# A four-stage transformer kernel: bias rows in four row groups, attention factors by row block, later waits in the delta stage

## The chip, the cores and the metric

The kernel runs on one NeuronCore of a Trainium2 chip. The core has five engines that run their own instruction streams and meet at semaphores: TensorE (PE; its weight loads are listed as PEld), VectorE (DVE), ScalarE (ACT), GpSimd (POOL) and SyncE (SP), which here only issues DMAs. The metric is the device time of one launch in microseconds (us), lower is better. Everything is fp32.

## The reference

The input is 2048 tokens of 512 numbers. Four residual layers follow each other, each on a layer-normalized input:

```python
x = x + attention_a(layernorm(x))   # channel attention: 512 x 512 scores
x = x + ffn(layernorm(x))           # six routed experts weighted by softmax of the top 6 of 8, plus a shared expert
x = x + attention_b(layernorm(x))   # gated delta rule with causal convolutions, 16 heads of 128
x = x + ffn(layernorm(x))           # the same weights again

# attention_a
attn_scores = einsum('bes,bfs->bef', qT, kT) / sqrt(16); softmax over f; @ vT; transpose; @ Wo
# ffn, last lines
eo = einsum('tnh,nhd->tnd', h, Wdown) + bdown
routed_out = einsum('tnd,tn->td', eo, w)
share = silu(xf @ Ws_up + bs_up) @ Ws_down + bs_down
```

## The kernel before

Each layer is a stage with its own semaphores; between stages all engines meet at a barrier. The order of the work on each engine is written out by hand in one block per engine, and each engine runs it strictly in that order.

**Attention factors** (`attention_stage`, from L215). Attention over channels needs no scores over tokens: the norm stage has accumulated the Gram matrix of the normalized input in PSUM banks 4 to 7, its upper triangle only. ScalarE copies the triangle out (L298), TensorE transposes the six missing 128 x 128 blocks (L270), ScalarE copies these (L301). Then come four products of 512 x 512 by 512 x 512, each as 4 x 4 matmuls of 128 x 512: `T1 = G Wk`, `S = Wq^T T1`, softmax over rows to `P`, `R1 = P^T Wo`, `M = Wv R1`. `product` (L260) has the output block `e` outside and the contraction block `k` inside, so one output bank after another is finished. ScalarE copies each finished bank to SBUF (L304, L311, L314); VectorE takes the row maxima of S (L321 to L323), ScalarE the exponentials (L307), VectorE scales by the reciprocal sums (L326, L328). Each product waits until all four blocks of its input are in SBUF (`pe.wait_ge(..., KC)`). Last, M is applied to the 16 token tiles (L291).

**Expert stages** (`ffn_stage`, L338, run twice). The 2048 tokens go through in FN = 4 blocks of 512. For each block there are 16 units: four chunks of the shared expert, then six experts of two chunks. `up(v)` (L428, L432) makes gate and up projections of unit v, ScalarE and VectorE form the hidden tile, `down(v - 1)` (L450) accumulates into PSUM banks 4 to 7, one bank for each 128 tokens. After the last unit of a block four more matmuls add the bias rows (L457): their contraction runs over 7 rows only, the six routed weights of a token and a row of ones, against `bdown` (six expert biases and the shared one). VectorE then adds the four banks to the residual (L552). TensorE's order at such a boundary is: shared up of the next block (its first unit), last down, four bias matmuls, shared up of the next unit, first down of the next block, which waits for the adds (`acc_read`). There are eight bias groups, three in the middle of each expert stage and one at each end.

**Delta stage** (`delta_stage`, L666). SyncE first issues the loads in this order: `xt` (first 512 tokens, transposed), `wab`, four projection weights `wqkv`, `wfb`, `par`, `dconst`, `onw`, then the second `xt`, `wgb`, `wo`, `xr`. GpSimd clears five buffers (L784 to L788) and signals `const_ready` after the last. TensorE waits for `const_ready` and `dconst` before its first matmul, which is `fa`, the low-rank decay projection (L1448, from `xt` and `wab`); ScalarE waits for `par` (L810) before it can copy `fa` out (L865); then TensorE makes the decay projection (L1442, from `wfb`) and the first q, k, v projections (L1367). The stage's loop runs over 16 units of 16 slots, with preparation two units ahead.

Of the kernel before, what the change touches and what calls it, by code (L numbers as in the profile page):

```python
# [8 lines left out]
ACT = mybir.ActivationFunctionType  # L9
# [224 lines left out]
def attention_stage(nc, x_sb, xnt, ps, cst, dram, ahead, meanvar):  # L234
# [3 lines left out]
    with ExitStack() as c2:  # L238
# [12 lines left out]
        with nc.Block() as block:  # L251
# [8 lines left out]
            def _(pe):  # L260
                def product(banks, lhs, rhs, signal):
                    for e in range(KC):
                        for k in range(KC):
                            last = pe.matmul(ps[:, banks + e, :], lhs[:, k, e * P:(e + 1) * P], rhs[:, k, :],
                                             start=(k == 0), stop=(k == KC - 1))
                        last.then_inc(signal, 1)
                for e in range(1, KC):
                    pe.wait_ge(g_upper, e)
                    for f in range(e):
                        last = pe.transpose(ps[:, e, f * P:(f + 1) * P], g[:, f, e * P:(e + 1) * P], cst[:, K_ID:K_ID + P])  # L270
                    last.then_inc(g_turned, 1)
                pe.wait_ge(w_in["wk"], 16)
                pe.wait_ge(g_upper, KC)
                pe.wait_ge(g_ready, KC - 1)
                product(0, g, w["wk"], t1_ps)
                pe.wait_ge(w_in["wq"], 16)
                pe.wait_ge(t1_ready, KC)
                product(4, w["wq"], t1, s_ps)
                pe.wait_ge(w_in["wo"], 16)
                pe.wait_ge(p_ready, KC)  # L280
                product(0, pr, w["wo"], r1_ps)
                pe.wait_ge(w_in["wvt"], 16)
                pe.wait_ge(r1_ready, KC)
                product(4, w["wvt"], r1, m_ps)
# [11 lines left out]
            def _(act):  # L296
                for e in range(KC):
                    act.activation(g[:, e, e * P:D], ps[:, 4 + e, e * P:D], ACT.Copy).then_inc(g_upper, 1)  # L298
                for e in range(1, KC):
                    act.wait_ge(g_turned, e)  # L300
                    act.activation(g[:, e, 0:e * P], ps[:, e, 0:e * P], ACT.Copy).then_inc(g_ready, 1)  # L301
# [37 lines left out]
def ffn_stage(nc, tag, x_sb, xnt, ps, cst, dram, store_to, wg, wu, wgu_in, meanvar=None):  # L339

    with ExitStack() as c2:
# [10 lines left out]
        bd = sb("bdown", [NR + 1, D])  # L352
        wt = sb("weights_t", [NE, T])
# [12 lines left out]
        names = ("w_in", "wr_in", "wd_in", "wsu_in", "wsd_in", "wt_out", "order", "logits_ps", "logits_out", "logits_turned", "logits_max",  # L366
                 "exp_ready", "probs_ready", "wt_ps", "wt_ready", "acc_ps", "acc_read", "stored", "gated")
        (w_in, wr_in, wd_in, wsu_in, wsd_in, wt_out, order, logits_ps, logits_out, logits_turned, logits_max, exp_ready, probs_ready, wt_ps,
# [11 lines left out]
        with nc.Block() as block:  # L380

            @block.sync
            def _(sp):
# [3 lines left out]
                for dst, name in ((bg, "bgate"), (bu, "bup"), (bs, "bsup"), (bd, "bdown")):  # L387
                    sp.dma_start(dst[:], dram[name]).then_inc(w_in, 16)
                sp.dma_start(wsd[:], dram["wsdown"]).then_inc(wsd_in, 16)
# [1209 lines left out]
```

## Time and profile before

| | |
|---|---|
| median of three runs | 3613.39 us (3612.41 to 3616.37) |
| the profiled execution | 3611.68 us, span 3609.6 us |
| granted TensorE clock, mean | 0.972 of full speed |
| TensorE busy | 3428.2 us, 95% of the span |
| VectorE, ScalarE busy | 1886.7 us (52%), 1434.1 us (40%) |
| matmuls of the bias rows, L457 | 64 records, 30.5 us busy |
| attention stage | from 57.6 to 186 us |
| expert stages | from 202.5 to 840 us and from 2971.8 us to the end |
| delta stage | from 861.2 to 2940.9 us |

"Busy" is the time in which at least one instruction of the engine ran. Each fp32 matmul stands in the trace as two records (4 bias matmuls are "x8"). "Granted clock" is the share of full TensorE speed; 1.00 is 2.4 GHz and 0.50 is 1.2 GHz. A name behind "<-" in brackets says what ended an idle time.

### The profile page before, as it was taken

The page shows a single profiled execution, that of the slowest core. Times are in us where ns is not written, and L with a number is a line of the kernel's source. Part 1 is how long each engine was busy: PE and PEld are TensorE (multiplying, and loading weights), DVE is VectorE, ACT ScalarE, POOL GpSimd, SP SyncE. Part 2 cuts the span into 40 slices and gives each one's busy share as a digit, 9 for nine tenths or more (in the row PEclk, how much of TensorE's full clock was granted, in tenths as well). Part 3 has the DMA queues.
Part 4 walks back from the last instruction along what each step waited for, and adds up shares of the span by engine and source line. Part 5 has one row for each costly group of instructions (what it writes and reads, how often), then busy time and mean ns, then how long its engine had stood idle before and what let it go on. Part 6 is the DMA issues. An engine that isn't in the chain of part 4 may idle for free. (4 is left out here: it accounts for less than half of the span.)

```text
span 3609.6 us, 85178 instructions
## 1 busy us (share of the span) xinstructions
PE 3428.2 (95%) x37232; PEld 1644.9 (46%) x37232; DVE 1886.7 (52%) x3186; ACT 1434.1 (40%) x3321; POOL 125.2 (3%) x457
## 2 busy tenths in 40 slices
PE   7989999996789999999999999999999869999999
PEld 4444444443344444454545454444445434444444
DVE  2221111113787888788877878887888431111111
ACT  2020000003357656766675676567666521000000
POOL 0000000000000000000000000000000000000000
PEclk9999999998889999999999999999999969999999
DMA  4030100004101111121111211111211032100000
GB/s 166 0 96 0 29 29 0 12 0 151 34 26 37 46 55 37 41 65 41 31 65 38 63 34 49 40 39 39 67 40 35 17 144 80 29 0 29 0 12 12
DMA packets 83725, 156.21 MB, mean 43 GB/s; under 512 B 8782, under 2 KB 33998, under 8 KB 79516
## 3 DMA queue, kind: packets, MB, share of 16 engines
q1 hardware_dynamic: 83356, 150.77, 12.9%
q8 instruction: 295, 4.83, 0.5%
q14 instruction: 74, 0.61, 0.1%
HBM read 133.71 MB, written 17.04 MB: 42 GB/s over the span
## 5 line engine op out<-in xcount | busy, mean ns | idle before, releaser
L1367 PE MATMUL psum<-dl_xt,dl_wqkv 128*128 128x512 f32 x1536 | 779.0, 625 | 9.6 <-DVE dl_qkv L1010 9.6
L541 DVE SCALAR_TENSOR_TENSOR f_act_g<-psum,f_bup,f_act_g 128x512 f32<-128x512 f32 x96 | 72.1, 751 | 929.8 <-ACT f_act_g L495 929.8
L1010 DVE SCALAR_TENSOR_TENSOR dl_qkv<-psum,dl_par,dl_qkv 128x511 f32<-128x511 f32 (+2 forms) x576 | 428.6, 744 | 39.0 <-ACT dl_tails L857 32.0
L495 ACT ACTIVATE f_act_g<-psum,f_bgate 128x512 f32<-128x512 f32 x96 | 66.0, 687 | 923.1 <-PE psum L432 923.1
L1367 PEld LDWEIGHTS psum<-dl_xt,dl_wqkv 128*128 128x128 f32 x1536 | 258.6, 190 | 249.7 <-issue 213.8
L432 PE MATMUL psum<-xnt_sb,wup 128*128 128x512 f32 x768 | 345.3, 593 | 0.0
L428 PE MATMUL psum<-xnt_sb,wgate 128*128 128x512 f32 x768 | 345.3, 593 | 0.0
L450 PE MATMUL psum<-f_wdown,f_hidden 128*128 128x512 f32 x768 | 345.0, 593 | 0.0
L1374 PE MATMUL psum<-dl_wo,dl_sg 128*128 128x512 f32 x512 | 261.0, 624 | 0.4 <-DVE dl_sg L1214 0.4
L853 ACT ACTIVATE dl_qkv<-psum,dl_par 128x512 f32<-128x512 f32 x192 | 148.8, 775 | 218.6 <-PE psum L1367 218.2
L428 PEld LDWEIGHTS psum<-xnt_sb,wgate 128*128 128x128 f32 x768 | 146.2, 190 | 183.4 <-issue 183.4
L450 PEld LDWEIGHTS psum<-f_wdown,f_hidden 128*128 128x128 f32 x768 | 146.2, 190 | 183.4 <-issue 183.4
L432 PEld LDWEIGHTS psum<-xnt_sb,wup 128*128 128x128 f32 x768 | 146.1, 190 | 183.4 <-issue 183.4
L1099 DVE TENSOR_TENSOR dl_kq<-dl_kq,dl_dec 128x512 f32<-128x512 f32 x320 | 206.9, 688 | 3.9 <-PE psum L1417 3.9
L823 ACT ACTIVATE dl_sdec<-dl_alt,dl_tot 128x128 f32<-128x128 f32 x512 | 162.5, 392 | 60.3 <-DVE dl_alt L1004 60.3
L838 ACT ACTIVATE dl_ubuf<-psum 128x128 f32<-128x128 f32 x256 | 70.4, 275 | 273.3 <-PE psum L1336 273.3
L823 ACT ACTIVATE dl_sdec<-dl_state,dl_tot 128x128 f32<-128x128 f32 x512 | 162.8, 395 | 21.8 <-DVE dl_state L1004 21.8
L1004 DVE TENSOR_TENSOR dl_alt<-dl_sdec,psum 128x512 f32<-128x512 f32 x128 | 87.5, 684 | 151.2 <-PE psum L1347 151.0
L1347 PE MATMUL psum<-dl_ubuf,dl_kkt 32*128 32x128 f32 x2048 | 132.3, 328 | 17.4 <-ACT dl_ubuf L838 17.4
L1417 PEld LDWEIGHTS psum<-dl_kq,dl_qkv 128*32 128x32 f32 x10240 | 106.9, 112 | 88.2 <-issue 82.3
L1004 DVE TENSOR_TENSOR dl_state<-dl_sdec,psum 128x512 f32<-128x512 f32 x128 | 87.5, 683 | 107.3 <-PE psum L1347 106.3
L997 DVE SCALAR_TENSOR_TENSOR dl_rbuf<-psum,dl_nkap,dl_val 128x128 f32<-128x128 f32 x256 | 87.9, 343 | 101.7 <-PE psum L1309 101.7
(200 smaller groups left out, 4494.0 us busy)
## 6 DMA issues: line engine op xcount, KB each, us to landing
dl_wqkv<-in_dw_qkv SPq DMA_DIRECT2D x192, 256.0 KB, 2.6
dl_wo<-in_dwo SPq DMA_DIRECT2D x16, 1024.0 KB, 6.2
f_weights_b<-f_weights_by_expert SPq DMA_DIRECT2D x48, 256.0 KB, 6.3
wgate<-in_wgate SPq DMA_DIRECT2D x2, 3072.0 KB, 19.3
wup<-in_wup SPq DMA_DIRECT2D x2, 3072.0 KB, 24.4
f_wdown<-in_wdown SPq DMA_DIRECT2D x2, 3072.0 KB, 13.0
x_sb<-in_x SPq DMA_DIRECT2D x4, 1024.0 KB, 9.2
x_after_experts<-x_sb SPq DMA_DIRECT2D x16, 256.0 KB, 2.0
```

Of the source, the lines that this page charges most:

```text
L428: last = pe.matmul(ps[:, 2 * b, :], lhs, xnt[:, k, s * FT:(s + 1) * FT], start=(k == 0), stop=(k == KC - 1))
L432: last = pe.matmul(ps[:, 2 * b + 1, :], wu[:, n, k, c * P:(c + 1) * P], xnt[:, k, s * FT:(s + 1) * FT], start=(k == 0), stop=(k == KC - 1))
L450: last = pe.matmul(ps[:, 4 + i, :], hid[:, b, i * P:(i + 1) * P], rhs, start=(u == 0), stop=False)
L823: last = act.activation(sdec[:, j, :], heads_state(k, sl)[:, j, :], ACT.Copy, scale=tot(k)[:, j, sl:sl + 1])
L853: act.activation(qkv[:, a, j, :], ps[:, bank, :], ACT.Identity, bias=par[:, h, 12 + a:13 + a], scale=par[:, h, 4 * a + 3:4 * a + 4])
L1004: dve.tensor_tensor(heads_state(k, sl + 1), sdec[:, :, :], ps[:, 0:HJ, 0:P], ALU.add).then_inc(s["s_read"], 1)
L1010: tap_ = lambda dl: dve.scalar_tensor_tensor(y_[:, dl:TT], ps[:, bank, 0:TT - dl], par[:, h, 4 * a + 3 - dl:4 * a + 4 - dl], y_[:, dl:TT], ...
L1099: o.done(dve.tensor_tensor(late, late, dv[:, :, :, 0, 0:1].broadcast_to([P, HJ, nb, m]), ALU.mult))
L1347: last = pe.matmul(ps[:, j, 0:P], kkt(k)[part(j), sl, :], ubuf[part(j), sl % 2, :], start=True, stop=True)
L1367: last = pe.matmul(ps[:, bank, :], wq[:, n % RING, m, :], xt[:, u // HG % 2, m, :], start=(m == 0), stop=(m == KC - 1))
L1374: last = pe.matmul(ps[:, bank, :], sg[:, m, P * i:P * i + P], wo[:, m, :], start=(m == 0), stop=(m == HJ - 1))
L1417: last = pe.matmul(ps[part(j), bank, C * g:C * g + C], chunk(qkv[:, KK], g)[:, j, :], rhs, start=True, stop=True)
```

## The change

Three edits, each in a stage of its own.

1. Expert stages: `bdown` and the transposed routing weights are loaded four times, to partitions 0, 32, 64 and 96, and bias matmul i takes its 7 rows from group i. ScalarE waits for three small loads instead of four; TensorE waits for the eight loads (`bd_in`) before the first bias group. SyncE issues three more `bdown` and three more `weights_t` DMAs per stage.
2. Attention: `product` does one contraction block k for all four banks at a time, and each k waits only for its own block of the input. The transposes of G move behind the wait for `wk`, between the blocks of the first product, and use bank 4.
3. Delta stage: SyncE waits for `xt` and `wab` to land before it issues the other loads; `const_ready` and `dconst` are waited for where they are used (TensorE from iteration k = -1 on); a new `tails_ready` covers the first cleared buffer alone.

```diff
@@ attention_stage, tensor engine
-                def product(banks, lhs, rhs, signal):
+                def product(banks, lhs, rhs, k, signal):
                     for e in range(KC):
-                        for k in range(KC):
-                            last = pe.matmul(ps[:, banks + e, :], lhs[:, k, e * P:(e + 1) * P], rhs[:, k, :],
-                                             start=(k == 0), stop=(k == KC - 1))
-                        last.then_inc(signal, 1)
-                for e in range(1, KC):
+                        last = pe.matmul(ps[:, banks + e, :], lhs[:, k, e * P:(e + 1) * P], rhs[:, k, :],
+                                         start=(k == 0), stop=(k == KC - 1))
+                        if k == KC - 1:
+                            last.then_inc(signal, 1)
+
+                def turn(e):
                     pe.wait_ge(g_upper, e)
                     for f in range(e):
-                        last = pe.transpose(ps[:, e, f * P:(f + 1) * P], g[:, f, e * P:(e + 1) * P], cst[:, K_ID:K_ID + P])
+                        last = pe.transpose(ps[:, 4, P * f:P * f + P], g[:, f, e * P:(e + 1) * P], cst[:, K_ID:K_ID + P])
                     last.then_inc(g_turned, 1)
                 pe.wait_ge(w_in["wk"], 16)
-                pe.wait_ge(g_upper, KC)
-                pe.wait_ge(g_ready, KC - 1)
-                product(0, g, w["wk"], t1_ps)
+                for k in range(KC):
+                    pe.wait_ge(g_upper, k + 1)
+                    if k > 0:
+                        pe.wait_ge(g_ready, k)
+                    if k + 1 < KC:
+                        turn(k + 1)
+                    product(0, g, w["wk"], k, t1_ps)
                 pe.wait_ge(w_in["wq"], 16)
-                pe.wait_ge(t1_ready, KC)
-                product(4, w["wq"], t1, s_ps)
+                for k in range(KC):
+                    pe.wait_ge(t1_ready, k + 1)
+                    product(4, w["wq"], t1, k, s_ps)
...
@@ ffn_stage
-        bd = sb("bdown", [NR + 1, D])
-        wt = sb("weights_t", [NE, T])
+        bd = sb("bdown", [P, D])
+        wt = sb("weights_t", [P, T])
...
+                for i in range(4):
+                    sp.dma_start(bd[32 * i:32 * i + NR + 1, :], dram["bdown"]).then_inc(bd_in, 16)
...
+                for i in range(4):
+                    sp.dma_start(wt[32 * i:32 * i + NE, :].rearrange("e (i t) -> e i t", t=P),
+                                 wt_dram.rearrange("i e t -> e i t")).then_inc(bd_in, 16)
...
                         if s == 0:
-                            pe.wait_ge(w_in, 16 * 5)
+                            pe.wait_ge(bd_in, 16 * 8)
                         for i in range(4):
-                            pe.matmul(ps[:, 4 + i, :], wt[0:NR + 1, s * FT + i * P:s * FT + (i + 1) * P], bd[:, :],
+                            rows = slice(32 * i, 32 * i + NR + 1)
+                            pe.matmul(ps[:, 4 + i, :], wt[rows, s * FT + i * P:s * FT + (i + 1) * P], bd[rows, :],
                                       start=False, stop=True).then_inc(acc_ps, 1)
@@ delta_stage, sync engine
                 sp.dma_start(xt[:, 0], xnt_dram[0]).then_inc(s["xt_in"], 16)
                 sp.dma_start(wab[:], d["dwa"]).then_inc(s["wab_in"], 16)
+                sp.wait_ge(s["xt_in"], 16)
+                sp.wait_ge(s["wab_in"], 16)
                 for n in range(RING):
                     load_proj(n)
@@ delta_stage, GpSimd; ScalarE and VectorE wait for tails_ready in place of const_ready at their start
-                pool.memset(tails[:], 0.0)
+                pool.memset(tails[:], 0.0).then_inc(s["tails_ready"], 1)
@@ delta_stage, tensor engine
-                pe.wait_ge(s["const_ready"], 1)
-                pe.wait_ge(s["dc_in"], 16)
                 for k in range(-2, UNITS + 1):
                     run = 0 <= k < UNITS
+                    if k == -1:
+                        pe.wait_ge(s["const_ready"], 1)
+                        pe.wait_ge(s["dc_in"], 16)
```

TensorE's stream in the attention stage, one piece of the difference (`at_t` is T1, `at_g` is G, `at_pr` is P, `at_r` is R1; 128x128 is a transpose):

```order
-L270 MATMUL psum<-constants_sb,at_g 128x128 x6
-L264 MATMUL psum<-at_wk,at_g 128x512 x16
-L264 MATMUL psum<-at_t,at_wq 128x512 x16
-L264 MATMUL psum<-at_wo,at_pr 128x512 x16
-L264 MATMUL psum<-at_r,at_wvt 128x512 x16
-L291 MATMUL psum<-at_m,xnt_sb 128x512 x64
+L271 MATMUL psum<-constants_sb,at_g 128x128
+L263 MATMUL psum<-at_wk,at_g 128x512 x4
+L271 MATMUL psum<-constants_sb,at_g 128x128 x2
+L263 MATMUL psum<-at_wk,at_g 128x512 x4
+L271 MATMUL psum<-constants_sb,at_g 128x128 x3
+L263 MATMUL psum<-at_wk,at_g 128x512 x8
```

The six transposes now stand between the row blocks of the first product; the counts of matmuls are the same.

SyncE's stream at the start of the delta stage, with waits, before. A semaphore of this stage is printed under the name that its number bore in an earlier stage, where there was one.

```order
L728 DMA dl_xt<-xn_transposed 128x2048
L729 DMA dl_wab<-in_dwa 128x1088
L726 DMA dl_wqkv<-in_dw_qkv 128x512 x4
L732 DMA dl_wfb<-in_dwfb 128x512
L733 DMA dl_par<-in_dheads 128x272
```

And now (`n1_std_ready` is here the semaphore of `wab`):

```order
L741 DMA dl_xt<-xn_transposed 128x2048
L742 DMA dl_wab<-in_dwa 128x1088
L739 DMA dl_wqkv<-in_dw_qkv 128x512 [waits n1_std_ready,dl_xt_in]
L739 DMA dl_wqkv<-in_dw_qkv 128x512 x3
L747 DMA dl_wfb<-in_dwfb 128x512
L748 DMA dl_par<-in_dheads 128x272
```

Twelve loads that were queued at once (four `wqkv`, then eight others) stand behind a wait now, `wfb` and `par` among them.

TensorE's stream at the same place, with waits, before (`n1_var_ready` stands for `wab`, `n1_xn_ready1` for `dconst`, `n1_dve_order` for `const_ready`):

```order
L1448 MATMUL psum<-dl_xt,dl_wab 128x512 [waits n1_var_ready,dl_xt_in,n1_xn_ready1,n1_dve_order]
L1448 MATMUL psum<-dl_xt,dl_wab 128x512 x3
L1442 MATMUL psum<-dl_fa,dl_wfb 128x512 [waits dl_read6,dl_wfb_in]
L1442 MATMUL psum<-dl_fa,dl_wfb 128x512 [waits dl_read6]
L1367 MATMUL psum<-dl_xt,dl_wqkv 128x512 [waits dl_w_in0,dl_xt_in]
```

And now:

```order
L1465 MATMUL psum<-dl_xt,dl_wab 128x512 [waits dl_xt_in,n1_std_ready]
L1465 MATMUL psum<-dl_xt,dl_wab 128x512 x3
L1459 MATMUL psum<-dl_fa,dl_wfb 128x512 [waits dl_read6,dl_wfb_in]
L1459 MATMUL psum<-dl_fa,dl_wfb 128x512 [waits dl_read6]
L1384 MATMUL psum<-dl_xt,dl_wqkv 128x512 [waits dl_w_in0,dl_xt_in]
```

The first matmul waits for its two operands alone; `dconst` and the cleared buffers are waited for later.

## Rows read from the trace of the kernel before

**Rows 1.** windows: stretch, length, busy us (instructions) by engine, granted clock, DMA share, GB/s
```profile
202.50:840.00 637.50, 630.32 (x1477) 276.15 (x1477) 101.10 (x159) 48.73 (x69) 0.00 (x0) 0.99 0.08 25
```

**Rows 2.** timeline (start us, us, engine, operation, tiles), TensorE, a boundary between token blocks
```profile
3135.78 3.70 PE L457 MATMUL psum<-f_bdown,f_weights_t 7*128 7x512 f32 x8
3139.41 5.40 PE L428 MATMUL psum<-xnt_sb,f_wsup 128*128 128x512 f32 x8
3144.64 3.60 PE L450 MATMUL psum<-f_wsdown,f_hidden 128*128 128x512 f32 x8
```

**Rows 3.** timeline, TensorE, another boundary, first expert stage
```profile
683.69 3.70 PE L428 MATMUL psum<-xnt_sb,f_wsup 128*128 128x512 f32 x8
687.23 3.60 PE L450 MATMUL psum<-f_wsdown,f_hidden 128*128 128x512 f32 x8
```

**Rows 4.** windows, columns as in rows 1, behind three bias groups of the first expert stage
```profile
367.90:374.70 6.80, 6.80 (x9) 2.52 (x8) 4.49 (x11) 0.00 (x0) 0.00 (x0) 0.50 0.62 172
528.30:531.70 3.40, 3.40 (x5) 1.35 (x4) 2.66 (x8) 0.00 (x0) 0.00 (x0) 0.50 0.50 152
683.70:690.00 6.30, 6.30 (x16) 2.95 (x16) 3.75 (x9) 0.69 (x1) 0.00 (x0) 1.00 0.33 122
```

**Rows 5.** timeline, TensorE, one state step of the delta stage and its successor
```profile
1770.24 0.50 PE L1347 MATMUL psum<-dl_ubuf,dl_kkt 32*128 32x128 f32 x8
1770.68 1.12 PE L1374 MATMUL psum<-dl_wo,dl_sg 128*128 128x512 f32 x2
```

**Rows 6.** timeline, VectorE: a PSUM add and successor; first output add behind rows 2
```profile
132.17 0.69 DVE L332 TENSOR_TENSOR x_sb<-psum,x_sb 128x512 f32<-128x512 f32 x1 [34.99 <-PE psum L291]
132.89 0.69 DVE L334 BATCH_NORM_STATS2 at_stats<-x_sb 128x6 f32<-128x512 f32 x1
...
3136.94 0.69 DVE L552 TENSOR_TENSOR x_sb<-psum,x_sb 128x512 f32<-128x512 f32 x1 [9.08 <-PE psum L457]
```

**Rows 7.** timeline, TensorE: first down projection of the first expert stage
```profile
217.33 3.24 PE L450 MATMUL psum<-f_wsdown,f_hidden 128*128 128x512 f32 x7 [0.16 <-DVE f_logits L519]
```

**Rows 8.** timeline, TensorE, the factors of the attention stage
```profile
58.31 1.20 PE L270 MATMUL psum<-constants_sb,at_g 128*128 128x128 f32 x6 [2.38 <-ACT at_g L298]
62.86 16.28 PE L264 MATMUL psum<-at_wk,at_g 128*128 128x512 f32 x32 [3.35 <-DMA at_wk<-in_wk]
79.92 13.97 PE L264 MATMUL psum<-at_t,at_wq 128*128 128x512 f32 x32 [0.78 <-ACT at_t L304]
97.32 15.67 PE L264 MATMUL psum<-at_wo,at_pr 128*128 128x512 f32 x32 [3.44 <-DVE at_pr L328]
113.77 13.97 PE L264 MATMUL psum<-at_r,at_wvt 128*128 128x512 f32 x32 [0.78 <-ACT at_r L311]
```

**Rows 9.** timeline, VectorE, softmax: last maximum, first and last scaling
```profile
93.92 0.69 DVE L321 TENSOR_REDUCE at_mx<-psum 128x1 f32<-128x512 f32 x1 [2.55 <-PE psum L264]
...
94.91 0.49 DVE L328 TENSOR_SCALAR at_pr<-at_pr,at_rc 128x512 f32<-128x512 f32 x1
...
96.69 0.49 DVE L328 TENSOR_SCALAR at_pr<-at_pr,at_rc 128x512 f32<-128x512 f32 x1
```

**Rows 10.** delta stage start: timelines of four engines, transfer window, landing of dl_xt
```profile
871.55 0.23 ACT L810 ACTIVATE dl_nega<-dl_par 128x16 f32<-128x16 f32 x1 [8.96 <-DMA dl_par<-in_dheads]
...
872.26 5.75 PE L1448 MATMUL psum<-dl_xt,dl_wab 128*128 128x512 f32 x8 [17.54 <-DMA dl_dconst<-in_dconst]
878.87 1.96 PE L1442 MATMUL psum<-dl_fa,dl_wfb 128*128 128x512 f32 x4 [0.86 <-ACT dl_fa L865]
...
861.31 0.33 SPq L728 DMA_DIRECT2D dl_xt<-xn_transposed  x1
...
863.00:865.00 2.00, 0.00 (x0) 0.00 (x0) 0.00 (x0) 0.00 (x0) 2.00 (x3) 0.50 0.93 385
...
DMA to landing us min/median/max: 4.9/7.1/9.3
...
865.10 0.53 POOL L788 MEMSET dl_xcr<- 128x512 f32 x1
```

More of the change, by code:

```diff
@@ L279, in _ @@
                 pe.wait_ge(w_in["wo"], 16)
-                pe.wait_ge(p_ready, KC)
-                product(0, pr, w["wo"], r1_ps)
+                for k in range(KC):
+                    pe.wait_ge(p_ready, k + 1)
+                    product(0, pr, w["wo"], k, r1_ps)
                 pe.wait_ge(w_in["wvt"], 16)
-                pe.wait_ge(r1_ready, KC)
-                product(4, w["wvt"], r1, m_ps)
+                for k in range(KC):
+                    pe.wait_ge(r1_ready, k + 1)
+                    product(4, w["wvt"], r1, k, m_ps)
@@ L300, in _ @@
                     act.wait_ge(g_turned, e)
[L301 removed]
+                    act.activation(g[:, e, 0:e * P], ps[:, 4, 0:e * P], ACT.Copy).then_inc(g_ready, 1)
                 for e in range(KC):
@@ L365, in ffn_stage @@
         cmp_a, cmp_b = (wb[:, 0, 2 * n:2 * n + 2, :].rearrange("p a (b c d) -> p (a b) c d", c=NE, d=NE) for n in range(2))
-        names = ("w_in", "wr_in", "wd_in", "wsu_in", "wsd_in", "wt_out", "order", "logits_ps", "logits_out", "logits_turned", "logits_max",
+        names = ("w_in", "bd_in", "wr_in", "wd_in", "wsu_in", "wsd_in", "wt_out", "order", "logits_ps", "logits_out", "logits_turned", "logits_max",
                  "exp_ready", "probs_ready", "wt_ps", "wt_ready", "acc_ps", "acc_read", "stored", "gated")
-        (w_in, wr_in, wd_in, wsu_in, wsd_in, wt_out, order, logits_ps, logits_out, logits_turned, logits_max, exp_ready, probs_ready, wt_ps,
+        (w_in, bd_in, wr_in, wd_in, wsu_in, wsd_in, wt_out, order, logits_ps, logits_out, logits_turned, logits_max, exp_ready, probs_ready, wt_ps,
          wt_ready, acc_ps, acc_read, stored, gated) = (sem(tag + n) for n in names)
@@ L386, in _ @@
                 sp.dma_start(wsu[:], dram["wsup"]).then_inc(wsu_in, 16)
-                for dst, name in ((bg, "bgate"), (bu, "bup"), (bs, "bsup"), (bd, "bdown")):
+                for dst, name in ((bg, "bgate"), (bu, "bup"), (bs, "bsup")):
                     sp.dma_start(dst[:], dram[name]).then_inc(w_in, 16)
+                for i in range(4):
+                    sp.dma_start(bd[32 * i:32 * i + NR + 1, :], dram["bdown"]).then_inc(bd_in, 16)
                 sp.dma_start(wsd[:], dram["wsdown"]).then_inc(wsd_in, 16)
@@ L483, in _ @@
                 act.activation(act_g[:, 0, :], ps[:, 4, :], ACT.Copy).then_inc(logits_out, 1)
-                act.wait_ge(w_in, 16 * 4)
+                act.wait_ge(w_in, 16 * 3)
                 for v in range(ALL):
@@ L699, in delta_stage @@
         b_dram = nc.dram_tensor("betas", [H, TT], F32).ap()
-        names = """const_ready wab_in par_in onw_in dc_in kps r_ready u_ps u_ready s_ps s_read sd_ready o_ps o_read o_squared tapped
+        names = """tails_ready const_ready wab_in par_in onw_in dc_in kps r_ready u_ps u_ready s_ps s_read sd_ready o_ps o_read o_squared tapped
             bnd_ready edged q_silu k_silu v_silu k_square q_square softplus_abs softplus_exp softplus_ln series_done softplus_sum decay_ready
@@ L813, in _ @@
                 act.wait_ge(s["nega_ready"], 1)
-                act.wait_ge(s["const_ready"], 1)
+                act.wait_ge(s["tails_ready"], 1)
                 def decay_state(k, sl):
@@ L818, in decay_state @@
                     if sl == 0:
+                        act.wait_ge(s["const_ready"], 1)
                         act.wait_ge(s["tot_ready"], k + 1)
@@ L986, in _ @@
                 step = lambda ins: (o.done(ins), o.wait())
-                dve.wait_ge(s["const_ready"], 1)
+                dve.wait_ge(s["tails_ready"], 1)
                 dve.wait_ge(s["dc_in"], 16)
@@ L1109, in level_take @@
                         wait_full(dve, "level", u, 0)
+                        dve.wait_ge(s["const_ready"], 1)
                         dve.tensor_copy(waited[:, 1:2], cst[:, K_ONE:K_ONE + 1])
```

1 line of the change is left out of this document (removed).

## The prediction

> **What bounds the kernel now.** I read the windows by stage first: in the first expert stage TensorE is busy 630 of 637.5 us at a granted clock of 0.99 [rows 1], and the second stands the same, so there every matmul that takes less time shortens the run one for one, and so does a stretch at half clock. Then the timeline at the edges, where work of TensorE is thin or absent: the boundary between two blocks of tokens [rows 2 to 4], the attention factors [rows 8, 9] and the start of the delta stage [rows 10]. The reader is to see three things. At a boundary the four bias matmuls (8 records) take as long as four full ones, though only 7 of the 128 rows work, and in five of six boundaries the following shared up projection takes longer than 3.5 us, 5.2 in the rows shown. In the attention stage TensorE stands still before each product, longest, 3.44 us, for the softmax. In the delta stage it starts only when `dconst` has landed, a table it doesn't use there.
>
> **Bias groups.** From the first bias record to the next projection a group takes 3139.41 - 3135.78 = 3.63 us [rows 2]. Records of a full matmul follow each other in 3.43 / 8 = 0.43 us (8 records from 683.69 to 687.23 are 3.54, with 0.11 of start). If four row groups run side by side, two record times stay and six go: 3.63 - 6 x 0.43 = 1.05 us. Do they? The trace has the case with 128 columns in place of 512: a state step sends four matmuls with 32 rows each to four banks, 8 records, and the next operation starts 0.44 us after the first of them [rows 5]. A record of 128 columns takes a quarter of 0.43, 0.107 us; one after the other the 8 would need 0.86. So they overlap fully, with about 0.2 us for the start and end. I take 1.07 us, a gain of 2.56 a group. The other bound is that accumulating groups go one by one: gain 0.
>
> In the middle of a stage (6 groups) the whole gain counts if the adds keep up. The first add starts 1.16 us after the first bias record in the old order (3136.94 behind 3135.78) [rows 2, 6]; the four banks are now complete at that same moment, and PSUM adds follow each other in 0.72 us (132.17 to 132.89) [rows 6], so they are done by 1.16 + 3 x 0.72 + 0.69 = 4.0 us. The next down projection, which overwrites the banks one each 0.86 us, comes one shared up (3.43) behind the group, at 4.5 us. It doesn't wait. 6 x 2.56 = 15.4 us.
>
> At the end of a stage (2 groups) the adds are the chain: the last began 3 x 0.86 us behind the first, paced by the matmuls, and begins 3 x 0.72 behind it now, 0.4 us sooner, 0.8 in both. Bias groups: 16.2 us.
>
> The Trainium skill speaks against counting the full factor (TensorEngine Tiling, PSUM Bottleneck: behind a fourfold speedup of TensorE, the copies out of PSUM may become the bound). By it the six inner groups would gain little; the row pitch of 0.72 us agrees at the two ends only.
>
> The added loads hide: the three more `bdown` issues come before `wsdown`, at some 0.45 us each, but the first down projection that needs it is released by VectorE's logits [rows 7]; without that cover they would cost 1.4 us per stage. The `weights_t` copies are wanted 100 us later. Nothing is taken for them.
>
> **The clock behind the bias groups.** Behind the first group of the first expert stage the granted clock is 0.50 for 6.8 us, behind the second for 3.4 us, behind the third it stays at 1.00 [rows 4]. Half clock for x us costs x / 2: 5.1 us together. In the second expert stage all three fall, as the one shown: 3144.64 - 3139.41 = 5.23 us against 3.54 without a fall [rows 2, 3], 1.7 each, 5.1. Since 3.6 us of seven-row matmuls is sometimes not enough for a fall, I expect none behind 1.07 us. Gain 10.2 us; bounds 0 and 10.2.
>
> The Trainium skill (TensorE: Matmul & The Clock Gate, What's actually happening) has the gate follow how busy TensorE has been. Read literally, the bias groups are busy all the time and the fall isn't theirs. The rows speak against this: each fall stands right behind seven-row matmuls. Were the page's reading right, the 10.2 us would stay lost.
>
> **Attention.** G's blocks are ready long before `wk` lands (the transposes end at 59.5, the product starts at 62.86, released by the load) [rows 8], so starting the first product on a part of G gains nothing, and the six transposes, which were hidden, now stand behind the load. They took 1.20 us with their waits; I take 0.8 for them back to back, partly at half clock (bounds 0.6 and 1.2): a loss.
>
> The second and fourth product each waited 0.78 us (plus a start of about 0.15) for the last copy [rows 8]. With k outside, the four banks finish 0.86 us apart in the last block, each copy is shorter than that, and the next product needs only the first. Gain 2 x 0.93 = 1.9.
>
> The softmax: the last bank is finished at 93.9 as before, but the other three only 2.6, 1.7 and 0.9 us earlier, so VectorE has a queue: four rounds of maximum and negation of 0.92 us each (0.69 + 0.15 and two starts), beginning at 91.35, end at 95.0. Then the first reciprocal and scaling, ready 0.6 us on, at 95.6, and the product may start on block 0 at 95.7; before, it needed the last scaling, which began at 96.69, and started at 97.32 [rows 8, 9]. Gain 1.6; the other scalings come 0.6 us apart, beneath blocks of 3.4 us. The old pause of 3.44 us was followed by a fall of the clock: the third product took 15.67 us, the second 13.97. A pause of 1.8 us should be survived more often than not; I take the 1.7 (bounds 0 and 1.7). Sum for the stage: 0.8 lost, 1.9 + 1.6 + 1.7 won: 4.4 us.
>
> **Delta stage.** `xt` lands 4.9 us after its issue at 861.3, at 866.2. `wab`, 0.56 MB behind it in the queue at 385 GB/s [rows 10], lands at 867.7. TensorE then starts `fa` at 867.8 and not at 872.26. Cold as before, it takes 5.75 us or up to one more: ready by 873.6 to 874.8.
>
> What is queued behind SyncE's new wait: twelve loads, and ScalarE waits for `par` before it can copy `fa` out. Before, `par` landed at 871.5, 10.2 us behind the first issue at 861.3, with 3.06 MB up to its end, 7.9 us at 385 GB/s; 2.3 us are latency. Now four `wqkv`, `wfb` and `par`, 1.45 MB, take 3.8 us behind 867.8, and with the latency `par` lands at 873.9. `nega` takes 0.5 us, so `fa` can be copied from 874.4, and with its own end in the middle of its range I take 874.6; the decay projection starts at 875.3, not at 878.87 [rows 10]. Gain 3.6 us, bounds 2.5 and 4.5. `par` is what is late next: without SyncE's wait the gain would be 0.5 more. Everything behind comes from that chain (the first convolution stood at 885 and needs `onw`, now at about 875.5) and moves with it. The last initial load lands 2 us later than before, some 8 us ahead of the first reuse of the `wqkv` ring. The last clearing ends at 865.6 [rows 10], so moving `const_ready` is worth nothing; the repeated waits are passed at once.
>
> **Sum.** 16.2 + 10.2 + 4.4 + 3.6 = 34.4 us. The profiled execution took 3611.7 us, so 3577.3; the median of the runs shown is 1.7 above it, so I predict 3579 us.
>
> **Rivals.**
> - *The clock still falls* (the bias groups or the softmax pause are not what drops it, or even the short ones are enough). For it: the pauses move but don't vanish. Against it: the third group of 3.6 us without a fall. 34.4 - 10.2 - 1.7 = 22.5 us: 3591.
> - *The row groups go one after another*, since they add to what stands in the banks, which the state step doesn't. Then groups cost 3.6 us and the clock falls: 34.4 - 26.4 = 8.0: 3605. Against it: four different banks, as in rows 5.
> - *The adds become the bound* inside the stages, by the page cited. The six inner groups would bring 0.4 us each like the ends, 13.0 less: 3592. Against it: adds need to begin 2.6 us later than in the sum before bank after bank is missed.
> - *Slower*: each change of row group empties the array and exposes the next weight load. A change of tiling costs about 0.1 us on each side; with weight load and fill it would be 0.6 us at all 8 records, 5.0 + 0.6 = 5.6 us a group in place of 3.6: 16 lost and not 16.2 won, and the longer thin stretch would keep the clock at half twice as long everywhere (another 6 to 10 lost, and the 10.2 not won). With the 8.0 of the rest: some 15 us slower, 3628. It decides from 4.6 us a group.
>
> **Chances and range.** Forecast 0.71, clock 0.13, adds 0.03, one by one 0.07, slower 0.03, others 0.03. The clock's falls in the delta stage depend on where pauses come to lie, and each is worth 1.7 us, so the forecast alone spans 3573 to 3586; with the clock rival the range is 3572 to 3593. What differs by under 0.2% (7.2 us) can't be told from no change. Faster: the first three and most of the fourth, 0.93; same 0.04; slower 0.03.
>
> **What would show it.** Bias groups: 8 records within 1.3 us, and the next shared up within 3.6 us of its start at all six boundaries. Attention: no idle before the second and fourth product, 1.8 us before the third. Delta stage: first matmul 4.4 us earlier against SyncE's first load, second projection 3.6. I am wrong if a bias group takes over 2 us, if the clock falls behind it, or if the delta stage does not shorten by 2.5 to 4.5 us from its first load to its end.

## The result and the profile after

The changed kernel takes 3578.04 us (median of 4 runs, 3575.09 to 3582.45) against 3612.9 us before, measured beside it (4 runs, 3610.29 to 3616.37): a ratio of 0.9903, 95% interval 0.989 to 0.9917. Measured once more it was 3579.93 us against 3613.2 us, ratio 0.9908 (0.9895 to 0.9922). The forecast was 3579 us. In the profiled executions the span goes from 3609.6 to 3580.5 us.

The timeline of TensorE in the changed kernel, at the first boundary between two blocks of tokens in the first expert stage and at the one that answers to [rows 2] (columns as there):

```profile
360.80 1.14 PE L470 MATMUL psum<-f_bdown,f_weights_t 7*128 7x512 f32 x8
361.87 3.70 PE L440 MATMUL psum<-xnt_sb,f_wsup 128*128 128x512 f32 x8
365.41 3.60 PE L462 MATMUL psum<-f_wsdown,f_hidden 128*128 128x512 f32 x8
...
3119.41 1.14 PE L470 MATMUL psum<-f_bdown,f_weights_t 7*128 7x512 f32 x8
3120.48 3.70 PE L440 MATMUL psum<-xnt_sb,f_wsup 128*128 128x512 f32 x8
```

A bias group now takes 1.07 us to the next projection, where [rows 2] has 3.63, and that projection takes 3.54 us (361.87 to 365.41) at the first place, where [rows 2] has 5.23. Windows behind three boundaries of the first expert stage, which answer to [rows 4]:

```profile
361.00:374.00 13.00, 13.00 (x37) 5.54 (x34) 5.54 (x12) 1.37 (x2) 0.00 (x0) 1.00 0.66 198
513.00:525.00 12.00, 12.00 (x34) 5.17 (x34) 5.55 (x12) 0.88 (x2) 0.00 (x0) 1.00 0.75 192
666.00:679.00 13.00, 13.00 (x37) 5.62 (x30) 5.54 (x12) 1.38 (x2) 0.00 (x0) 1.00 0.22 81
```

The granted clock is 1.00 in all of them. It fell at five of six boundaries before, at none now.

The gain in an expert stage can be read without the noise of the whole time. From the start of the first bias group of a stage to the start of its fourth it is 466.28 and 466.33 us before (365.24 to 831.52, 3135.78 to 3602.11) and 453.57 us in both stages now (360.80 to 814.37, 3119.41 to 3572.98): 12.7 and 12.8 us. Both stages of e1 and of e9 to e12, further executions with the same bias groups, take 453.57 us too.

VectorE's adds behind the last bias group, of before (first fence) and after:

```profile
3603.27 0.69 DVE L552 TENSOR_TENSOR x_sb<-psum,x_sb 128x512 f32<-128x512 f32 x1 [5.65 <-PE psum L457]
...
3605.84 0.69 DVE L552 TENSOR_TENSOR x_sb<-psum,x_sb 128x512 f32<-128x512 f32 x1 [0.17 <-PE psum L457]
```

```profile
3574.14 2.48 DVE L565 TENSOR_TENSOR x_sb<-psum,x_sb 128x512 f32<-128x512 f32 x4 [5.65 <-PE psum L470]
```

Before, the adds were paced by the matmuls, one each 0.86 us, and took 3605.84 + 0.69 - 3603.27 = 3.26 us; now four stand back to back in 2.48 us, a pitch of (2.48 - 0.69) / 3 = 0.60 us.

The attention factors on TensorE, which answer to [rows 8], and the two rows of VectorE that answer to [rows 9]:

```profile
63.44 0.47 PE L271 MATMUL psum<-constants_sb,at_g 128*128 128x128 f32 x1 [7.22 <-DMA at_wk<-in_wk]
63.71 5.77 PE L263 MATMUL psum<-at_wk,at_g 128*128 128x512 f32 x8
...
73.30 7.03 PE L263 MATMUL psum<-at_wk,at_g 128*128 128x512 f32 x16
80.17 13.90 PE L263 MATMUL psum<-at_t,at_wq 128*128 128x512 f32 x32
95.72 13.97 PE L263 MATMUL psum<-at_wo,at_pr 128*128 128x512 f32 x32 [1.66 <-DVE at_pr L336]
109.53 13.90 PE L263 MATMUL psum<-at_r,at_wvt 128*128 128x512 f32 x32
124.11 6.28 PE L299 MATMUL psum<-at_m,xnt_sb 128*128 128x512 f32 x14 [0.69 <-ACT at_m L322]
```

```profile
95.09 0.49 DVE L336 TENSOR_SCALAR at_pr<-at_pr,at_rc 128x512 f32<-128x512 f32 x1
...
96.87 0.49 DVE L336 TENSOR_SCALAR at_pr<-at_pr,at_rc 128x512 f32<-128x512 f32 x1
```

No row of the second or fourth product has idle time; the third starts 0.63 us behind the start of the first scaling and 1.15 us ahead of the last one. Its pause is 1.66 us and not 3.44, and it takes 13.97 us and not 15.67, so the clock didn't fall.

The start of the delta stage, which answers to [rows 10]: timelines of TensorE, ScalarE and SyncE, then windows of the transfers.

```profile
849.82 5.33 PE L1465 MATMUL psum<-dl_xt,dl_wab 128*128 128x512 f32 x8 [12.67 <-DMA dl_wab<-in_dwa]
858.65 2.45 PE L1459 MATMUL psum<-dl_fa,dl_wfb 128*128 128x512 f32 x4 [3.49 <-ACT dl_fa L881]
```

```profile
857.40 0.23 ACT L825 ACTIVATE dl_nega<-dl_par 128x16 f32<-128x16 f32 x1 [12.96 <-DMA dl_par<-in_dheads]
857.66 0.22 ACT L827 ACTIVATE dl_nega<-dl_nega 128x16 f32<-128x16 f32 x1
857.91 0.60 ACT L881 ACTIVATE dl_fa<-psum 128x512 f32<-128x512 f32 x1
```

```profile
843.15 0.33 SPq L741 DMA_DIRECT2D dl_xt<-xn_transposed  x1
843.53 0.43 SPq L742 DMA_DIRECT2D dl_wab<-in_dwa  x1
849.85 1.76 SPq L739 DMA_DIRECT2D dl_wqkv<-in_dw_qkv  x4
851.65 0.43 SPq L747 DMA_DIRECT2D dl_wfb<-in_dwfb  x1
852.12 0.43 SPq L748 DMA_DIRECT2D dl_par<-in_dheads  x1
```

```profile
851.00:853.00 2.00, 2.00 (x4) 0.85 (x3) 0.00 (x0) 0.00 (x0) 0.00 (x0) 0.50 1.03 289
853.00:855.00 2.00, 2.00 (x5) 0.57 (x3) 0.00 (x0) 0.00 (x0) 0.00 (x0) 0.96 0.77 236
855.00:857.00 2.00, 0.16 (x1) 0.00 (x0) 0.00 (x0) 0.00 (x0) 0.00 (x0) 1.00 0.90 305
```

TensorE starts early, as meant: 6.67 us behind SyncE's first load and not 10.95. But SyncE then stands until 849.85, ScalarE's first use of `par`, which comes right behind its landing, is only 14.25 us behind the first load (10.24 before), ScalarE has waited 12.96 us for it, and TensorE 3.49 us for ScalarE. The decay projection comes 15.50 us behind the first load, 17.56 before; the first convolution on VectorE, which is the end of this chain, at 23.50 and 23.86.

Where the time went, by windows of the whole run, cut at SyncE's first load of the delta stage and its last store, of before and after:

```profile
0.00:861.30 861.30, 811.78 (x2059) 372.77 (x2059) 170.47 (x315) 95.58 (x154) 0.20 (x4) 0.98 0.12 41
861.30:2935.40 2074.10, 1971.39 (x33632) 985.03 (x33632) 1607.27 (x2688) 1277.87 (x3077) 125.01 (x453) 0.97 0.14 45
2935.40:3609.60 674.20, 645.07 (x1541) 287.06 (x1541) 109.00 (x183) 60.65 (x90) 0.00 (x0) 0.97 0.12 41
```

```profile
0.00:843.10 843.10, 794.62 (x2059) 365.93 (x2059) 169.47 (x315) 96.11 (x154) 0.20 (x4) 0.98 0.13 42
843.10:2917.50 2074.40, 1972.73 (x33632) 985.78 (x33632) 1607.85 (x2688) 1278.68 (x3077) 124.99 (x453) 0.97 0.14 45
2917.50:3580.50 663.00, 630.68 (x1541) 281.24 (x1541) 107.96 (x183) 60.77 (x90) 0.00 (x0) 0.97 0.13 42
```

18.2 us were won ahead of the delta stage (attention, three bias groups inside the expert stage and one at its end), 11.2 behind it, and in the delta stage nothing: 2074.1 and 2074.4 us.

### The profile page after: what moved, and what is told of

The parts are those of the page before. It is cut to its first block and busy times, and to the rows that moved or that the text cites. A ratio compares the mean times of both kernels' runs of the same rounds, so it can differ in the third digit from the quotient of the medians.

```text
span 3580.5 us, 85211 instructions
## 1 busy us (share of the span) xinstructions
PE 3398.0 (95%) x37232; PEld 1633.0 (46%) x37232; DVE 1885.3 (53%) x3186; ACT 1435.6 (40%) x3321; POOL 125.2 (3%) x457
```

## The experiments

Theory: the bias groups (by their own time and by the clock) and the attention edit bring the time, as the forecast has it; the delta edit brings its 3.6 us, or its wait takes them back. The rivals of the forecast are tested with it. The kernel before was run beside each group of runs: 3612.51 us (27 runs) beside e1 to e4, 3612.31 (21 runs) beside e5 to e8, 3613.2 (9 runs) beside e9 to e12. Ratios are to these.

**The three parts alone.** e1 is the kernel before with the bias edit of the diff (L397, L413 and L469), e2 with the attention edit, e3 with the delta edit.

> The kernel before with the bias edit alone (four row groups). Theory: the row groups run side by side (8 records within 1.14 us, a group of 1.07 us in place of 3.63) and the clock no longer falls behind a group: 16.2 + 10.2 = 26.4 us less, 3586 to 3588. Rival 1, the clock gain comes from somewhere else than the bias groups: 16 us less, and the shared up projection behind a group takes 5.2 us at most boundaries. Rival 2, part of the gain is eaten by the added loads: under 24 us.

> The kernel before with the attention edit alone. Theory: 4.4 us less with the clock kept behind the softmax pause, 2.7 if it falls. The trace has no idle before the second and fourth product and 1.7 to 1.9 us before the third. Rival, the six transposes now behind the load of wk cost more than the overlap of the copies brings: 2 us less or nothing.

> The kernel before with the delta edit alone. The theory of the prediction: 3.6 us less. Rival, from the trace of the changed kernel: SyncE's wait holds par back, fa stands finished 3.5 us before ScalarE may copy it out, TensorE's clock falls in that pause, and the first convolution comes only 0.4 us earlier: 0 to 0.5 us less, and the delta stage as long as before (2074 us from its first load to its last store).

Measured: e1 3586.42 us (5 runs, ratio 0.9930, 0.9916 to 0.9944); e2 3608.37 (11 runs, 0.9992, 0.9983 to 1.0001); e3 3610.75 (11 runs, 0.9998, 0.9989 to 1.0006). The bias edit carries 26.1 us; from the first to the fourth bias group of a stage e1 takes 453.57 us in both stages, the same as the changed kernel. The attention edit's interval reaches from 6.1 us won to nothing, so the whole time doesn't show it. The traces do: the first bias group of the first expert stage, which has only the norm and the attention stage and the same expert work ahead of it, starts between 365.2 and 366.5 us in the seven profiled executions without the attention edit (before, e1, e3 to e6, e8) and between 360.4 and 362.4 in the four with it (e2, after, e9, e11): means 366.1 and 361.1, 5.0 us. The delta edit can't be told from none by the whole time, nor from the 3.6 us of the forecast: its interval reaches 4.0 us won. The product of the three ratios is 0.9920, 4 to 6 us short of the whole; the intervals are just wide enough for that.

**e4: the delta edit without SyncE's waits.** It keeps the rest of the delta edit.

```diff
-                sp.wait_ge(s["xt_in"], 16)
-                sp.wait_ge(s["wab_in"], 16)
                 for n in range(RING):
                     load_proj(n)
```

> The delta edit without SyncE's two waits (TensorE's wait for dconst and the cleared buffers still moved). If SyncE's wait is what took the gain: par lands 10.2 us behind the first load as in the kernel before, fa (ready 12.5 us behind it) is copied at once, the decay projection starts 4.1 us earlier than before, and the run is 3.5 to 4.5 us shorter. Rival, the start of the stage is not on the path at all, later work absorbs it: as e3, no gain.

Measured 3609.74 us (11 runs, 0.9992, 0.9983 to 1.0001): 2.8 us less than before, under the 3.5 to 4.5 expected and not shown by the time alone. TensorE's timeline in e3, then in e4 (SyncE's first load at 863.21 and 861.09):

```profile
869.87 5.95 PE L1452 MATMUL psum<-dl_xt,dl_wab 128*128 128x512 f32 x8 [13.83 <-DMA dl_wab<-in_dwa]
877.95 3.60 PE L1446 MATMUL psum<-dl_fa,dl_wfb 128*128 128x512 f32 x4 [2.13 <-ACT dl_fa L868]
```

```profile
867.74 5.64 PE L1450 MATMUL psum<-dl_xt,dl_wab 128*128 128x512 f32 x8 [13.39 <-DMA dl_wab<-in_dwa]
874.24 1.95 PE L1444 MATMUL psum<-dl_fa,dl_wfb 128*128 128x512 f32 x4 [0.87 <-ACT dl_fa L866]
```

Both start `fa` some 6.65 us behind the first load: the early start doesn't come from SyncE's wait. With the wait the second projection is 14.74 us behind the load and takes 3.60 us at half clock; without it 13.15 and 1.95. The first convolution on VectorE follows at 22.68 and 19.45 (23.86 in the kernel before).

**e5: the bias matmuls with all 128 rows.** One row group, `bd` and `wt` cleared to zero by GpSimd and filled in their first rows, so that the same four matmuls run over 128 rows one after the other. It tells whether thin work lets the clock fall, or the boundary itself.

```diff
-        bd = sb("bdown", [NR + 1, D])
-        wt = sb("weights_t", [NE, T])
+        bd = sb("bdown", [P, D])
+        wt = sb("weights_t", [P, T])
...
-                            pe.matmul(ps[:, 4 + i, :], wt[0:NR + 1, s * FT + i * P:s * FT + (i + 1) * P], bd[:, :],
+                            pe.matmul(ps[:, 4 + i, :], wt[:, s * FT + i * P:s * FT + (i + 1) * P], bd[:, :],
```

> The kernel before, but the bias matmuls contract over all 128 rows: bdown and weights_t are cleared to zero first and only 7 rows carry numbers; still one matmul after another. If seven-row work is what lets the clock fall: a group takes 3.43 us, no fall behind the six inner groups, the shared up projection behind it takes 3.43 us, and the run is 10.2 us plus 6 to 8 times 0.2 us shorter, 3600 to 3602. Rival, the fall comes from VectorE's adds, the DMAs or the boundary as such: falls stay at most of the boundaries and the run is 1 to 2 us shorter, 3611.

Measured 3600.38 us (4 runs, 0.9965, 0.9952 to 0.9979). TensorE's timeline at its first boundary:

```profile
366.48 3.60 PE L464 MATMUL psum<-f_bdown,f_weights_t 128*128 128x512 f32 x8
369.91 3.60 PE L435 MATMUL psum<-xnt_sb,f_wsup 128*128 128x512 f32 x8
```

The group is as long as a full projection, and the projection behind it is at full clock. No clock falls at any of the six boundaries of this kernel. The median is 11.9 us lower, with an interval from 7.6 to 17.3. The traces are sharper: from the first bias group to the fourth e5 takes 460.07 us in both stages, 6.2 and 6.3 less than before, 12.5 in all. Of these 10.2 are the clock (the stretches of [rows 4] and their like); the rest is 0.4 us for each boundary, since a group takes 3.43 us and not 3.63, and the projections on both sides of it 3.43 and not 3.53.

Over all profiled executions: the clock fell at 29 of the 36 inner boundaries of the six kernels with seven rows in one group (before, e2, e3, e4, e7, e8), and at none of the 48 of the eight kernels with four or two row groups or with 128 rows.

**e6: two row groups.** e1 with the banks on two row groups in turn.

```diff
-                            rows = slice(32 * i, 32 * i + NR + 1)
+                            rows = slice(32 * (i % 2), 32 * (i % 2) + NR + 1)
```

> The bias edit with two row groups in place of four (matmul i takes group i % 2). If the time goes by record times side by side: 8 records in four of them, a group of 3.63 - 4 x 0.43 = 1.9 us, 1.7 won at six places, some 0.6 at the two ends, and the clock kept: 3613 - 10.3 - 0.6 - 10.2 = 3591. Rival, the second matmul of a group waits for its own row group and blocks those behind it, so nothing overlaps beyond the first pair: 2.6 to 3 us a group, 3600. If the clock falls behind some of the groups of 1.9 us, 1.7 more for each.

Measured 3588.91 us (4 runs, 0.9937, 0.9922 to 0.9953). TensorE's timeline at the first boundary of e6:

```profile
366.37 1.99 PE L462 MATMUL psum<-f_bdown,f_weights_t 7*128 7x512 f32 x8
368.29 3.70 PE L432 MATMUL psum<-xnt_sb,f_wsup 128*128 128x512 f32 x8
```

One group costs 3.63 us (before), two 1.92, four 1.07, and neither of the last two is followed by a fall. The gain goes by row groups side by side, as the sum took it, and the median is 2 us under the 3591 expected, within its interval.

**e7: attention edit, transposes first.** e2 with the six transposes ahead of the wait for `wk`, each row of blocks in a bank of its own, and the product started on the whole of G.

```diff
+                for e in range(1, KC):
+                    pe.wait_ge(g_upper, e)
+                    for f in range(e):
+                        last = pe.transpose(ps[:, e, f * P:(f + 1) * P], g[:, f, e * P:(e + 1) * P], cst[:, K_ID:K_ID + P])
+                    last.then_inc(g_turned, 1)
                 pe.wait_ge(w_in["wk"], 16)
```

> The attention edit with the six transposes ahead of the wait for wk, as in the kernel before, and the contraction outside. Theory: the transposes are hidden again; from the first product to the application of M 59.8 us (65.6 before, 60.7 in the changed kernel with 0.3 more ahead of it), the run 0.8 us shorter than with the attention edit alone, 3607.5. Rival, the copies of G are late without the blocks between: as the attention edit alone.

Measured 3607.47 us (11 runs, 0.9987, 0.9978 to 0.9996), as expected; here the interval excludes no change. What the order of the transposes adds is another matter. `wk` lands at another time in each execution, so it has to be read from that landing. From there to the application of M, which took 65.6 us before, the versions with transposes behind the load take 61.1 us (e2), 60.7 (the changed kernel), 60.6 (e9) and 60.8 (e11), those with transposes first 59.7 (e7), 60.4 (e10) and 60.0 (e12): some 0.8 us less, which is the term of 0.8 in the forecast.

**e8: delta edit, parameters first.** e3 without SyncE's waits and with `par` and `wfb` right behind `wab`.

```diff
-                sp.wait_ge(s["xt_in"], 16)
-                sp.wait_ge(s["wab_in"], 16)
+                sp.dma_start(par[:], d["dheads"]).then_inc(s["par_in"], 16)
+                sp.dma_start(wfb[:], d["dwfb"][0]).then_inc(s["wfb_in"], 16)
                 for n in range(RING):
                     load_proj(n)
-                sp.dma_start(wfb[:], d["dwfb"][0]).then_inc(s["wfb_in"], 16)
-                sp.dma_start(par[:], d["dheads"]).then_inc(s["par_in"], 16)
```

> The delta edit without SyncE's waits and with par and wfb issued right behind wab. Par lands some 8 us behind the first load, fa is ready later than that, so its landing no longer matters and this is like the variant without waits: decay projection 13 us behind the first load, the run 3 us shorter than before, 3609 to 3610. Rival, the first projection weights come too late now: the first convolution comes over 20 us behind the first load, 3611.

Measured 3610.77 us (11 runs, 0.9994, 0.9985 to 1.0003). `par` is there 6.66 us behind the first load, yet the first convolution comes at 19.55 and not sooner than in e4 (19.45): once `par` lands by 10.4 us (e4), the end of `fa` is what is late, not `par`. Moving the small loads ahead brought nothing beyond taking the wait out.

**The changed kernel and two variants of it.** e9 is the changed kernel itself, e10 has the edit of e7 on top, e11 that of e8, e12 both.

> The changed kernel once more, unaltered, as the yardstick for the three versions timed beside it. Both theories: 3576 to 3580 us (3578.0 before). The product of the ratios of its three parts timed alone (0.9930, 0.9992, 0.9998) is 0.9920, or 3583 to 3584; if it lands there instead, the first timing was a lucky one; if it stays at 3578, the parts help each other by some 5 us or the bias part alone was timed high.

> The changed kernel with the transposes of its first attention product issued ahead of the wait for the weight wk, into banks of their own, and the four mirror copies with them. Theory that savings ahead of the first normalised tile carry to the end: the fourth product ends 2.0 to 2.5 us sooner than in the changed kernel, and the time is 1 to 2.5 us under the yardstick. Rival, that a later drop of the clock or a load takes it back: no difference (within 1 us).

> The changed kernel without SyncE's two waits ahead of the projection weights, and with the per-head parameters and the decay weights issued right behind the first loads. Theory that the start of the delta stage is a chain that its end follows: parameters 6.7 us behind the first load instead of 14.3, first convolution at 19.5 instead of 23.5, and 2 to 4 us off the time. Rival, that the stage is paced further on (by the state steps and by the clock): the first convolution as early, but under 1.5 us off the time. The same edit on the kernel before gave 1.5 us, so 1 to 2 us is taken.

> Both edits of the two runs beside it together: early transposes and the order of the delta loads without SyncE's waits. Theory that they add: 2 to 4.5 us under the yardstick, 3574 to 3576 us. Rival, that the phase of the clock decides at this size: the best of the four by less than 1 us, or not the best.

Measured: e9 3579.93 us (4 runs, 3577.28 to 3581.89), e10 3578.95 (5 runs, 3576.98 to 3582.24), e11 3575.29 (4 runs, 3574.94 to 3580.64), e12 3576.92 (4 runs, 3574.51 to 3578.64); ratios 0.9908, 0.9908, 0.9899 and 0.9900, each some 0.0014 either way. e10 missed: the fourth product starts 0.2 us sooner than in e9 and not 2 (the expectation had read an early landing of `wk` into the gain). e11 came out 4.6 us under e9 where 1 to 2 were expected. e11 and e12 have the lowest medians, but their intervals overlap with e9's, so by time alone neither is shown to beat the changed kernel, and the two edits don't visibly add. The start of e11 on TensorE and ScalarE:

```profile
855.89 1.95 PE L1457 MATMUL psum<-dl_fa,dl_wfb 128*128 128x512 f32 x4 [0.87 <-ACT dl_fa L879]
```

```profile
850.14 0.23 ACT L823 ACTIVATE dl_nega<-dl_par 128x16 f32<-128x16 f32 x1 [5.78 <-DMA dl_par<-in_dheads]
...
855.14 0.60 ACT L879 ACTIVATE dl_fa<-psum 128x512 f32<-128x512 f32 x1 [4.53 <-PE psum L1463]
```

ScalarE now waits for TensorE, not for the load, and the pause of TensorE is 0.87 us. What tells the versions apart better than the whole time is the length of the delta stage, from SyncE's first load to its last store, one execution each:

| start of the delta stage | executions | length, us |
|---|---|---|
| as before | before, e1, e2, e5, e6, e7 | 2074.0, 2073.3, 2077.3, 2078.0, 2072.7, 2073.0 |
| as changed, SyncE waits | after, e3, e9, e10 | 2074.4, 2074.1, 2075.9, 2070.4 |
| SyncE doesn't wait | e4, e8, e11, e12 | 2069.7, 2070.8, 2068.8, 2071.9 |

The same start varies by 5 us. The clock is one reason: one minus the granted clock, summed over windows of 2.5 us of the stage, is 49.7 us in e6, the shortest of the six with the start as before, and 60.6 in e5, the longest. The four stages without SyncE's wait are all shorter than these six (means 2070.3 and 2074.7, 4.4 us), and the clock accounts for little of it (the sums have means of 52.9 and 54.2). Those of the changed start, with a mean of 2073.7, are not all shorter.

## Why the prediction came out right, and where it didn't

**Bias groups: right inside the stages, not at the ends.** 1.07 us a group, as taken, so 6 x 2.56 = 15.4 us. With the clock the sum had 12.8 us for each stage; 12.7 and 12.8 were measured. At the two ends the adds are done 3.26 - 2.48 = 0.78 us sooner each, more than the 0.4 taken, because the PSUM adds follow each other in 0.60 us: the pitch of 0.72 came from an add with another operation behind it [rows 6]. But the end of the kernel doesn't come sooner by it: it is 7.49 us behind the start of the last group before, and 7.52 to 7.60 in after, e1, e9 and e11. The four stores behind the adds take it back: each landed 2.0 us behind its issue, now 2.3 to 2.8. At the end of the first stage the way to SyncE's first load of the delta stage went from 29.79 to 28.78 us, but e1, with the same edit, has 29.88. So the term of 0.8 is not shown at either end.

**The clock behind them: right.** All 10.2 us came back, and e5 shows the cause by itself: seven working rows for 3.6 us let the clock fall, 128 rows for as long do not. One reading of the forecast was not exact: at the first boundary of the kernel before the fall comes inside the bias group, which takes 4.58 us and not 3.63:

```profile
365.24 4.64 PE L457 MATMUL psum<-f_bdown,f_weights_t 7*128 7x512 f32 x8
369.82 6.10 PE L428 MATMUL psum<-xnt_sb,f_wsup 128*128 128x512 f32 x8
```

The loss of 3.4 us that was taken there covers both rows, so the sum is not touched. The Trainium skill (TensorE: Matmul & The Clock Gate, What's actually happening) has the clock follow how busy TensorE has been. Read as time in which it is occupied, that doesn't agree with these rows: TensorE has no idle time in the groups, before or in e5.

**The adds don't become the bound: right.** The next shared up and the down behind it start on time at all six boundaries. The rival would have cost some 13 us; it doesn't bear here, since a shared up projection of 3.5 us stands between the group and the next use of its banks. The Trainium skill (TensorEngine Tiling, PSUM Bottleneck) says that behind a fourfold speedup of TensorE the copies out of PSUM may become the bound; inside the stages this trace doesn't show that.

**Attention: right in its sum, 4.9 for 4.4 us.** By the starts in [rows 8] and in the fence above: from `wk` to the second product 17.06 before and 16.73 now, won 0.3 (0.9 by the idle time less the transposes); to the third 17.40 and 15.55, won 1.85 (taken 1.6); to the fourth 16.45 and 13.81, won 2.64 (taken 1.7 + 0.93); to the last factor 14.66 and 14.58. `wk` landed 0.6 us later in this execution, which leaves 4.3 at the end. The clock survived the pause of 1.66 us in all seven profiled executions with the edit, where the third product takes 13.97 us; behind the pause of 3.44 us it fell in all seven without it (15.67 us).

**Delta stage: wrong.** The term was 3.6 us (bounds 2.5 and 4.5) and the condition for being wrong was a stage that doesn't shorten by 2.5: against the 2074.1 us of before it didn't in after, e3 and e9 (e10 has 2070.4). The first step held (`fa` 4.3 us sooner), and so did the one that what comes behind moves with this chain: in e4 the first convolution comes 4.4 us sooner. What failed is the price of SyncE's wait. By the sum `par` should land 12.6 us behind the first load; it took 14.25, 13.49, 13.56 and 13.08 in after, e3, e9 and e10. The rate of 385 GB/s [rows 10] was carried over to transfers that start anew behind a pause (14 GB/s between 849 and 851), and there it was 236 to 305 in after. The projection behind it came at 15.50 and 14.3 to 14.8, not 14.0, and TensorE's pause of 2.1 to 3.5 us was followed in after and e3 by a stretch at half clock, which the sum didn't have. The length of the pause alone doesn't tell where: the clock fell behind 2.13 us (e3) and 3.49 (after), and stayed behind 2.46 (e10) and 2.92 (e9). The prediction put the price of the wait at 0.5 us; e3 against e4 shows 1.6 us at the decay projection and 3.2 at the first convolution, and the table some 3.4 us in the stage. e9 and e10 kept the clock there and had the convolution at 21.1 and 20.6, yet their stages take 2075.9 and 2070.4 us: their sums of one minus the granted clock, 54.5 and 49.2 us, differ by nearly as much.

**The total: right in part by luck.** The traces of before and after add up so: 4.4 us up to the first bias group, 12.7 from it to the fourth, 1.0 from there to the delta stage, 0.3 lost in the delta stage, 1.4 lost between it and the first bias group of the second expert stage, 12.8 from there to its fourth and nothing behind it, 29.1 in all. The sum had 34.4; the 5.3 that are missing are the delta stage (3.9) and the norm and router of the second expert stage (1.4), where nothing was changed. The windows up to its first projection, before and after:

```profile
2935.35:2980.14 44.79, 19.56 (x96) 11.67 (x97) 20.16 (x56) 11.92 (x21) 0.00 (x0) 0.62 0.80 314
```

```profile
2917.53:2963.76 46.23, 20.48 (x96) 12.42 (x96) 20.25 (x56) 12.03 (x21) 0.00 (x0) 0.59 0.78 303
```

The granted clock is 0.59 against 0.62 and the stretch 1.4 us longer; in e9 it takes 44.7 us, as before, in e10 46.2. The profiled execution of the changed kernel was the slowest of its four runs; over the medians the gain is 33.3 to 34.9 us, some 4 to 6 more than these two traces hold. That the medians meet the forecast within 1 us though one term of 3.6 us was not found is therefore in part luck, and what makes up for the term can't be told from these runs.

## What to carry to other kernels

Matmuls with few rows cost twice here: their own time, and the half clock behind them. Putting them side by side in row groups of their own brought 25.5 us inside the stages, padding them with rows of zeros 12.5. A wait on the engine that issues the loads holds back every load behind it, also the small one that is wanted next (here `par`, 3.1 us later in e3 than in e4); look for that load before you add the wait. And a gain of a few us at one place is read from the starts of the instructions behind it, over several executions, since the whole time varies by as much.

## What the runs showed that was not expected

- 3.6 us of seven-row matmuls without any idle time between them let the granted clock fall to 0.50 (1.2 GHz) at five of six boundaries; the same with 128 rows, mostly zero, left it at 1.00 (2.4 GHz) at all six, and took 12.5 us less in the traces though more rows work.
- Four groups of seven rows and 512 columns, each adding to a bank that already holds a sum, take 1.07 us together, 1.92 in two turns, 3.63 one after the other.
- Adds that were done 0.78 us sooner at the end of the kernel brought nothing, because the stores behind them landed that much slower.
- Behind SyncE's pause the four projection weights and the small loads moved at 236 to 305 GB/s in after, and at 290 to 328 in e3 and e9; without it the same weights moved at 391 to 403 in e11:

```profile
849.00:851.00 2.00, 1.20 (x2) 0.69 (x3) 0.00 (x0) 0.44 (x2) 0.00 (x0) 0.50 1.05 403
851.00:853.00 2.00, 2.00 (x4) 0.83 (x3) 0.00 (x0) 0.00 (x0) 0.00 (x0) 0.53 1.06 391
```

TensorE is busy in the last of them, so its work is not what slows the loads; what does was not tried.
